# Cross-attention on one core: maxima subtracted by VectorE, sums kept by GpSimd, values projected about once a step, a last part in another order

## The reference, cut to what matters

```python
x = x + _L0_xattn_ref(_layernorm(x), ctx_1024, Wq1, Wk1, Wv1, Wk2, Wv2, Wo, bo)
x = x + _L0_attn_ref(_layernorm(x), ...)
x = x + _L0_ffn_ref(_layernorm(x), ...)

def _L0_xattn_ref(x1, x2, Wq1, Wk1, Wv1, Wk2, Wv2, Wo, bo):   # B=4, N1=256, N2=4096, D=256
    q1 = split_heads(x1 @ Wq1)                                # 8 heads of 64
    k = concat([split_heads(x1 @ Wk1), split_heads(x2 @ Wk2)])
    v = concat([split_heads(x1 @ Wv1), split_heads(x2 @ Wv2)])
    sim = einsum('bihd,bjhd->bhij', q1, k) * 64 ** -0.5
    attn = softmax(sim, axis=-1)
    out = einsum('bhij,bjhd->bihd', attn, v)
    return out.reshape(B, N1, 512) @ Wo + bo
```

## Time and profile before

| | us |
|---|---|
| median of 3 runs | 1660.13 |
| lowest, highest | 1657.44, 1663.04 |
| profiled execution, own time | 1661.31 |
| its span, first to last instruction | 1659.3 |
| granted TensorE clock, mean over the span | 0.961 |
| granted clock, 90 to 1160 us | 1.00 |

### The profile page before, as it was taken

One profiled execution on the slowest core, in us unless ns is written; L12 is line 12 of the kernel. 1 busy time (PEld: TensorE's weight loads), 2 busy tenths in 40 slices (PEclk: granted clock), 3 DMA queues, 4 the chain that ended last, 5 costly groups with the idle time before them and its releaser, 6 DMA issues. The chain is left out here.

```text
span 1659.3 us, 29603 instructions
## 1 busy us (share of the span) xinstructions
PE 1489.4 (90%) x11988; PEld 1121.4 (68%) x11988; DVE 1124.6 (68%) x1283; ACT 712.1 (43%) x971; POOL 443.8 (27%) x286
## 2 busy tenths in 40 slices
PE   4999999999999999999999999998597777827995
PEld 4877777776777777777777777766354444527995
DVE  2687578657657765865876685685676999644663
ACT  3443345443444543444454444333345333224773
POOL 4300003200000320100131000000133999433885
PEclk8999999999999999999999999999797999958998
DMA  5000021000002100000300000000304900092333
GB/s 174 14 11 11 1 84 51 1 14 11 11 15 87 36 2 14 20 1 27 99 11 2 23 11 2 2 1 1 84 10 178 231 0 0 1 362 63 63 59 58
DMA packets 62388, 76.50 MB, mean 46 GB/s; under 512 B 6385, under 2 KB 47985, under 8 KB 61857
## 3 DMA queue, kind: packets, MB, share of 16 engines
q1 hardware_dynamic: 57168, 68.51, 13.6%
q0 software_dynamic: 5088, 6.11, 2.5%
HBM read 58.39 MB, written 17.25 MB: 46 GB/s over the span
## 5 line engine op out<-in xcount | busy, mean ns | idle before, releaser
L537 DVE TENSOR_REDUCE xa_maxes<-psum 128x2 f32<-128x1024 f32 (+1 forms) x288 | 334.2, 1162 | 265.0 <-PE psum L741 264.9
L467 ACT ACTIVATE xa_probs<-psum 128x1024 f32<-128x1024 f32 x272 | 268.7, 1026 | 273.2 <-PE psum L774 272.8
L558 DVE TENSOR_TENSOR xa_prob_sum<-xa_prob_sum,xa_probs 128x1024 f32<-128x1024 f32 x240 | 313.1, 1305 | 11.3 <-ACT xa_probs L467 10.5
L786 PE MATMUL psum<-xa_probs,xa_vals 128*64 128x256 f32 x2176 | 280.5, 389 | 2.0 <-DVE xa_heads_T L572 1.5
L786 PEld LDWEIGHTS psum<-xa_probs,xa_vals 128*64 128x64 f32 x2176 | 139.4, 136 | 104.6 <-issue 41.8
L458 ACT ACTIVATE xa_vals<-psum 128x512 f32<-128x512 f32 x136 | 81.2, 597 | 207.6 <-PE psum L666 207.6
L768 PE MATMUL psum<-xa_q_hi,xa_k_hi 64*128 64x256 f32 x1088 | 156.4, 283 | 0.6 <-issue 0.6
L666 PE MATMUL psum<-xa_wv_hi,xa_ctx_hi 128*128 128x256 f32 x512 | 150.7, 294 | 4.4 <-DVE xa_maxes L537 4.4
L772 PE MATMUL psum<-xa_q_hi,xa_k_lo 64*128 64x256 f32 x1088 | 154.3, 279 | 0.0
L774 PE MATMUL psum<-xa_neg_max,xa_ones 64*128 64x256 f32 x1088 | 154.2, 279 | 0.0
L770 PE MATMUL psum<-xa_q_lo,xa_k_hi 64*128 64x256 f32 x1088 | 153.8, 278 | 0.0
(11 more groups left out here) (329 smaller groups left out, 3019.5 us busy)
## 6 DMA issues: line engine op xcount, KB each, us to landing
xa_ctx_in<-in_ctxT_dram SPq DMA_DIRECT2D x32, 512.0 KB, 3.8
ex_slots<-mx_blank_tile SPq DMA_DIRECT2D x2, 4372.5 KB, 37.5
xa_stage<-in_L_xattn_Wk_dram SPq DMA_DIRECT2D x32, 128.0 KB, 2.4
xa_stage<-in_L_xattn_Wv_dram SPq DMA_DIRECT2D x16, 256.0 KB, 3.1
ex_raw<-in_L_ffn_w_gate_dram SPq DMA_DIRECT2D x8, 512.0 KB, 10.1
ex_raw<-in_L_ffn_w_up_dram SPq DMA_DIRECT2D x8, 512.0 KB, 10.8
ex_raw<-in_L_ffn_w_down_dram SPq DMA_DIRECT2D x8, 512.0 KB, 11.6
ex_xt<-ex_slots SPq DMA_DIRECT2D x15, 265.0 KB, 2.8
```

Source lines behind the costliest of these rows:

```text
L467: nc.scalar.activation(probs[:, n % RING, :], S[:, 2 * (n % 2):2 * (n % 2) + 2, :].rearrange("p h q -> p (h q)"), ACT.Exp, scale=HD ** -0. ...
L537: dve.tensor_reduce(maxes[:, qt, :, g:g + 1], max_banks(v, g, qt)[:, :, 0:group_keys(g)[1]], AX_X, ALU.max).then_inc(max_reduced, 1)
L558: dve.tensor_tensor(prob_sum[:, :], prob_sum[:, :], probs[:, n % RING, :], ALU.add).then_inc(summed, 1)
L786: i = pe.matmul(O[half[h], 0:N1], vals[:, 2 * j + t, lanes:lanes + HD], probs[:, n % RING, (2 * h + t) * N1:(2 * h + t + 1) * N1], start=( ...
```

## The change

Parts of it, as the code shows them:

- The product of ones and negative maxima is gone. `turn_maxima` makes rows of the positive maxima for both heads (four products instead of two), `store_max` copies them to SBUF, and VectorE's `shift` subtracts them from a score tile on its way from PSUM to the ring in SBUF. The exponential then works in place in SBUF.
- `add_probs` moves from VectorE to GpSimd.
- `score` waits for `shift` of tile n - 2 instead of its exponential, and no longer for the maxima.
- ScalarE stores keys between the step's two exponentials.
- `v_due` gives values in other steps; loads and splits of value weights are moved to match. The load of a context chunk waits for the value products too.
- `project_queries(u + 2)` stands ahead of the last weighing.
- The last output projection is in two parts, three pairs of heads in step 2 of the last unit and the fourth at the end (`project_last`), in the M banks.
- The semaphores are cleared by four engines, a quarter each.

```diff
@@ v_due
             if u % 2 == 1 and u + 1 < U:
-                return [((u + 1) // 2, j) for j in (2 * d - 4, 2 * d - 3) if 0 <= j]
+                return [((u + 1) // 2, j) for j in ((5, 6) if d == STEPS - 1 else (d - 3,)) if j >= 0]
             if u % 2 == 0 and u > 0:
-                return [(u // 2, j) for j in (2 * d + 14, 2 * d + 15) if j < HG]
+                return [(u // 2, j) for j in ((7, 8) if d == 0 else (9, 10) if d == 1 else (9 + d,)) if j < HG]
@@ sync
-                if d == 0 and u % 2 == 0 and u + 2 < U:
-                    load_values(u // 2 + 1)
-                if d == 4 and u % 2 == 0 and u + 2 < U:
-                    load_pair(u + 2)
-                if d == 0 and u % 2 == 1 and u + 2 < U:
+                if d == 0 and u % 2 == 1 and u + 1 < U:
+                    load_values((u + 1) // 2)
+                if d == 0 and u + 2 < U:
                     load_pair(u + 2)
...
+                    sp.wait_ge(v_projected, u // 2 * HG + 2 * d + 3)
                     load_chunk(u // PAIRS + 1, d)
@@ gpsimd
-            pool.memset(max_cols[:, :, :], 0.0).then_inc(setup, 1)
...
+            def add_probs(u, j):
+                n = u * HG + j
+                pool.wait_ge(exp_done, n + 1)
+                if j == 1:
+                    if u > 0:
+                        pool.wait_ge(sums_ready, u)
+                    pool.tensor_tensor(prob_sum[:, :], probs[:, (n - 1) % RING, :], probs[:, n % RING, :],
+                                       ALU.add).then_inc(summed, 1)
+                else:
+                    pool.wait_ge(summed, sums_done(n) - 1)
+                    pool.tensor_tensor(prob_sum[:, :], prob_sum[:, :], probs[:, n % RING, :],
+                                       ALU.add).then_inc(summed, 1)
...
             for u, d in steps():
-                if d == 3 and u % 2 == 0 and u + 2 < U:
-                    split_values_weights(u // 2 + 1)
+                if d >= 1:
+                    add_probs(u, 2 * d - 1)
+                if d == STEPS - 1 and u + 2 < U:
+                    split_weights(u + 2)
+                if d >= 1:
+                    add_probs(u, 2 * d)
+                if d == 1 and u % 2 == 1 and u + 1 < U:
+                    split_values_weights((u + 1) // 2)
@@ scalar
-                if n >= RING:
-                    act.wait_ge(pv_done, n - RING + 1)
-                    act.wait_ge(summed, sums_done(n - RING))
-                act.wait_ge(scores_ready, n + 1)
-                nc.scalar.activation(probs[:, n % RING, :], S[:, 2 * (n % 2):2 * (n % 2) + 2, :].rearrange(
-                    "p h q -> p (h q)"), ACT.Exp, scale=HD ** -0.5).then_inc(exp_done, 1)
+                act.wait_ge(shifted, n + 1)
+                nc.scalar.activation(probs[:, n % RING, :], probs[:, n % RING, :], ACT.Exp,
+                                     scale=HD ** -0.5).then_inc(exp_done, 1)
...
-                for j in step_tiles(d):
-                    exponentials(u, j)
+                exponentials(u, 2 * d)
                 if d + 1 < NG and v < U:
                     store_k_hi(v, d + 1)
+                if d < STEPS - 1:
+                    exponentials(u, 2 * d + 1)
@@ vector
-                dve.tensor_scalar(neg_max[:, :], M[:, 1, 0:N1], -1.0, None, ALU.mult).then_inc(neg_max_ready, 1)
+                dve.tensor_copy(max_rows[:, :, :].rearrange("p h q -> p (h q)"), M[:, 1, :]).then_inc(max_ready, 1)
...
+            def shift(u, j):
+                n = u * HG + j
+                dve.wait_ge(scores_ready, n + 1)
+                if j == 0:
+                    dve.wait_ge(max_ready, u + 1)
+                if n >= RING:
+                    dve.wait_ge(pv_done, n - RING + 1)
+                    dve.wait_ge(summed, sums_done(n - RING))
+                dve.tensor_tensor(probs[:, n % RING, :].rearrange("p (h t q) -> p h t q", h=2, t=2),
+                                  S[:, 2 * (n % 2):2 * (n % 2) + 2, :].rearrange("p h (t q) -> p h t q", t=2),
+                                  max_rows[:, :, :].unsqueeze(2).broadcast_to([P, 2, 2, N1]),
+                                  ALU.subtract).then_inc(shifted, 1)
@@ tensor, turn_maxima
-                for qt in range(QT):
-                    i = pe.matmul(M[:, 1, qt * P:(qt + 1) * P], max_cols[:, qt, :], ident[:, :],
-                                  start=True, stop=True)
+                for h in range(2):
+                    for qt in range(QT):
+                        i = pe.matmul(M[:, 1, h * N1 + qt * P:h * N1 + (qt + 1) * P],
+                                      row_max[:, qt, h:h + 1].broadcast_to([P, P]), ident[:, :],
+                                      start=True, stop=True)
@@ score
-                    pe.wait_ge(exp_done, n - 1)
-                if j == 0:
-                    pe.wait_ge(neg_max_ready, u + 1)
+                    pe.wait_ge(shifted, n - 1)
...
-                        pe.matmul(out[h], k[2 + h], q[h], start=False, stop=False)
-                    for h in range(2):
-                        i = pe.matmul(out[h], ones[half[h], :], neg_max[half[h], :], start=False, stop=True)
+                        i = pe.matmul(out[h], k[2 + h], q[h], start=False, stop=True)
@@ steps of the tensor engine
                     score_for_max(v, d, 1, values)
+                    if u + 2 < U:
+                        project_queries(u + 2)
                     weigh(u, HG - 1)
                     for c, j in v_due(u, d):
                         project_values(c, j, maxima)
                         values += 1
-                    if u + 2 < U:
-                        project_queries(u + 2)
                     turn_maxima(v, values)
...
+                    if d == 2:
+                        project_last(range(IC - 1))
...
-            project_output(B - 1)
+            project_last(range(IC - 1, IC))
@@ end
-            for used in sems:
+            for used in sems[0::4]:
                 pool.sem_clear(used)
...
```

More of the change, by code:

```diff
@@ L403, in _ @@
                     split_query_weights(u + 2)
-                if d == STEPS - 1 and u + 2 < U:
-                    split_weights(u + 2)
         @block.scalar
@@ L575, in add_output @@
                 dve.wait_ge(out_projected, b + 1)
[L576 to L577 removed]
+                made = M[:, :, 0:D] if b == B - 1 else KQ.rearrange("p (t d) -> p t d", t=QT)
+                dve.tensor_tensor(X1[:, b * QT:(b + 1) * QT, :], made, X1[:, b * QT:(b + 1) * QT, :],
+                                  ALU.add).then_inc(x1_done, 1)
             dve.wait_ge(x_loaded, 16)
@@ L618, in _ @@
                     normalize(u - 1)
-                if d >= 2 and not (d == STEPS - 1 and v < U):
-                    add_probs(u, 2 * d - 1)
+                shift(u, 2 * d)
                 if v < U:
@@ L809, in project_output, with project_last @@
                 i.then_inc(out_projected, 1)
+            def project_last(pairs):
+                pe.wait_ge(o_normalized, (B - 1) * PAIRS + pairs[-1] + 1)
+                if pairs[0] == 0:
+                    pe.wait_ge(max_ready, U)
+                    pe.wait_ge(v_stored, U // 2 * HG)
+                for qt in range(QT):
+                    for c in pairs:
+                        i = pe.matmul(M[:, qt, 0:D], heads_T[:, c, qt * P:(qt + 1) * P],
+                                      wo_sb[:, c, :], start=(c == 0), stop=(c == IC - 1))
+                if pairs[-1] == IC - 1:
+                    i.then_inc(out_projected, 1)
             pe.wait_ge(ident_ready, 1)
             turn_own(0)
-            pe.wait_ge(setup, 3)
+            pe.wait_ge(setup, 2)
             project_queries(0)
@@ L883, in _ @@
         def _(pool):
-            for used in sems:
+            for used in sems[0::4]:
                 pool.sem_clear(used)
+        @block.sync
+        def _(sp):
+            for used in sems[1::4]:
+                sp.sem_clear(used)
+        @block.scalar
+        def _(act):
+            for used in sems[2::4]:
+                act.sem_clear(used)
+        @block.vector
+        def _(dve):
+            for used in sems[3::4]:
+                dve.sem_clear(used)
 def mixer(nc, w, X1, ident, psum, slots, held):
```

60 lines of the change are left out of this document (22 added, 38 removed).

## The result

The changed kernel takes 1653.5 us (median of 7 runs, 1652.8 to 1658.0) where the kernel before took 1660.0 (median of 7, 1657.4 to 1663.0): 0.9971 of it, with a 95% interval of 0.9961 to 0.9981, so some 5 us faster by the ratio and 6.5 by the medians, 0.3%. Forecast were 1647.0, 13 us less. The direction and the range held; half of the expected gain or more is missing. The profiled execution of the changed kernel took 1658.0 us, the highest of its seven, 3.3 less than the profiled one of before.

What follows compares the result with a forecast made beforehand. The prediction took TensorE (PE) work as the bound, a queue with almost no holes. Its terms, -4.6 - 5.1 - 2.4 (unit 0) - 0.8 = -12.9 us, gave 1648.4 profiled and a forecast of 1647, range 1612 to 1672.

Steps and rivals of the forecast that it cites:

- rival 3: VectorE's subtractions are blocked by GpSimd at 2.52 us each, in every step; slower, 1713 us; chance 0.08.
- rival 2: GpSimd becomes the bound, its sums taking 2.85 us beside context chunks and in the last unit; 1691 us; chance 0.12.
- Beginning of units: PE waits about 1.15 us for a late reduction in even units and again in odd ones: +2.3 a pair.
- Values 1.65 a pair: Value products stand in 14 places instead of 9 in a pair of units, at 0.33 us each: +1.65.
- GpSimd's give-back: VectorE's adds no longer slowed while GpSimd splits chunks: 1.7 us in each of three units, -5.1.
- Units 1 to 14: Seven pairs of cross-attention units: -4.6 us from PE's saving less new costs, and -5.1 from adds leaving VectorE.
- wait for the reduction: PE's second maxima product waits for VectorE's reduction, 0.17 us in 11 steps: +1.9 a pair.
- turn of the maxima: Turning maxima for both heads adds two small products a unit, 0.35 us: +0.7 a pair.
- queries: Moved ahead of the last weighing, they no longer fill PE's wait for the last values in odd units: +0.8 a pair.
- The last unit: GpSimd's sums end it, +4.7; output projection -2.8; semaphore clears -2.7; together -0.8 us.
- Rival 1: All of PE's saving comes through as waits in the unit pairs vanish: 35 us more, 1612 us; chance 0.15.
- Rival 4: New waits at the maxima (0.26 us) and units' beginnings (1.5 more a pair) eat the saving; 1664 us; chance 0.15.

Runs made afterwards that it cites:

- run 6: The changed kernel with GpSimd's sums of the exponentials formed over only 64 of 1024 columns; 1645.2 us.
- run 4: The changed kernel with the value products back in the steps where they stood before the change; 1644.4 us.
- run 2: The changed kernel with every other sum of the last unit back on VectorE; 1647.6 us.
- run 11: The changed kernel with both maxima reductions of each step reading only half of the keys; 1624.5 us.
- run 3: The changed kernel with the query product behind the values again, as before the change; 1648.9 us.
- run 9: The kernel before with only the change's end: output projection in two parts and semaphores cleared by four engines; 1656.1 us.
- Version 7: The changed kernel with alternate last-unit sums on VectorE, query product behind the values, and values in their old steps; 1632.6 us.
- run 1: The kernel before without the product of ones and negative maxima, so the maxima are not taken off the scores; 1627.7 us.
- run 8: Version 7 with the second maxima product behind the keys in steps without values, VectorE's order matched, one value product moved; 1652.5 us.
- run 12: Version 7 with the maxima product that opens the next step one weighing earlier in steps without values; 1638.7 us.

## Why the forecast was too large

Point by point, by the steps of its own sum.

*Held.* Step 7.5 us in odd and even units (7.54). Subtractions 1.2 us (1.216 over 272), with GpSimd at work for 63% of the span. The narrow form of the rule, of the Trainium skill's page SBUF — State Buffer, SBUF: two separate sides, agrees with this trace (one operand in PSUM, no blocking), and rival 3 fell with it. GpSimd's sums 2.4 us (2.39), its chunks in time, no wait of PE for it (run 6): rival 2 fell. Beginning of units 1.15 + 1.15 a pair: 1.1 at the value product in each even unit, 1.1 in step 2 of odd ones. Values 1.65 a pair: the traces of run 4 give 11.8 / 7 = 1.7. GpSimd's give-back: the units with chunks were 1.5 us longer than their like before (75.7 against 74.2) and have no such surplus now. Unit 0 gave 4.2, not 2.4, but it varies with the same code (53.0 us in the changed kernel's trace, 51.4 in run 2's), so this difference tells little.

*Units 1 to 14* came to -3.6 instead of -9.7, 6.1 us or 0.9 a pair, spread over terms that were each a little small. The **wait for the reduction** was put at 0.17 in 11 steps, as a delay of one product; it is 0.20, because the product after the late one is late too (run 11). The **turn of the maxima** for both heads was put at 0.35 a unit; it takes 0.89 instead of 0.4, so 0.5. The **queries** were put at 0.8 a pair; by the traces of run 3 they cost 7.8 / 7 = 1.1. Together 0.3 + 0.3 + 0.3 are the 0.9, within what the reading allows.

*The last unit* is the step that failed: forecast **-0.8**, measured +6.0. These 6.8 us and the 6.1 of units 1 to 14 are what the forecast had too much. Three terms of the last unit were mis-sized. The **sums "one behind the other at 2.35"** went by the length of one instruction; a chain in which each waits for the one before runs at 2.50 (35.05 / 14), and it starts 5.9 us after the row maxima and loses 0.9 at its second sum. It ends at 1119.27 + 35.05 = 1154.32, 47.0 us after the row maxima (1107.30), not 42.7: +4.3. The **output projection** was to fall by 2.8; from the last sum to X it is 7.1 us against 8.0 before, only 0.8 less. PE, without work while GpSimd adds, drops to the lower of its clocks (0.68, then 0.50 granted, about 1.2 of 2.4 GHz), and the short products behind the sums run at that: 2.17 us from the normalization to the sum into X instead of 1.22 (runs 9 and 6, granted clock 0.94 and 1.00 there). Runs 2 and 7 have the same code in the last unit, and their projection takes 1.14 us in the one (granted 0.87) and 2.08 in the other (0.50), so it is the clock and not the code. The term itself also took for granted that three quarters of the projection cost nothing in step 2. That holds here, where PE waits for GpSimd's sums, and not in the kernel before, where run 9 gains nothing by it. Moving the end's bound to another engine slowed the end of the engine that was left waiting. The **clears** gave 2.2 instead of 2.7.

6.1 + 6.8 us would bring -12.9 to 0; unit 0 (1.8 more than forecast), the start (+0.8) and the two later blocks (-2.9 and +0.8, the same code) bring the profiled execution to about -3.3. How much of the 6.5 us between the medians belongs to the change is therefore open.

*What the forecast could have seen.* It had the sum's parts with signs: four of the edits had only a price (values in more places, queries forward, maxima for two heads, sums on GpSimd in the last unit). Version 7 shows what it is worth to take three of these four out: 21 us. The forecast priced them and never asked whether the same gain was to be had without them.

*Rival 1*, all of the saving comes: no, run 1 shows that even alone half of it is lost. *Rival 4* (new waits, 1664): the waits were 0.20 and not 0.26 a step and did not grow at the units' beginnings, so it was not this. *The direction* came out right in part by luck: in the two traces units 1 to 15, for which -10.5 of the -12.9 were forecast, got 2.4 us longer together (-3.6 and +6.0), and what makes the execution shorter lies in unit 0 and in the mixer.

## What to carry to other kernels

When an instruction leaves a saturated engine, look at the engine that shares a buffer with it: the saving lasts up to that one's next completion, and a late product delays its follower too. Size a serial chain by the distance of starts, and at a block's end ask which engine is left idle and at what clock it does its last products. Work moved forward saves only where it lands on an engine with time to spare (run 9). Where a change bundles edits, run the costly ones backwards singly; here they added up (6 + 5 + 9 gave 21).

## What the runs showed of the hardware

- Adds of 128x1024 fp32 on GpSimd last 2.39 us but follow each other every 2.50 when each waits for the one before (14 in 35.05 us). VectorE's subtraction of the same size from PSUM takes 1.22 beside it (mean of 272).
- After GpSimd had left PE with little to do (4.05 us of 12 busy, clock 0.68), four products of 128x256 took 2.07 us at a granted clock of 0.50, and 1.13 in the kernel where PE had been busy (11.00 of 11 us, run 9, then 0.94). With the same code in the last unit they took 1.14 at 0.87 (run 2) and 2.08 at 0.50 (run 7).
- The first key product (128 rows) starts 0.21 us after the last score product (64 rows) in run 8 (529.53 to 529.74), where like score products and the maxima product behind them (64 rows too) start after 0.12 (run 12). So the order of a step seems to be worth tenths of a microsecond without any wait; no run tests it alone.
- A wait of 0.10 us for another engine, once a step, stands in no line of the waits: it shows only when the start of the product is set against the end of the reduction, and halving the reduction removed it (run 11). The 132 places of L753 that are put down to "issue" are others; run 11 has 129 of them still.
- 52 semaphores cleared by four engines take 1.72 to 2.08 us between blocks, by one engine 3.93.
